# A transformer block on one core: the cell's sigmoids kept in PSUM, the output's input product made late and four tiles at once, and new instruction orders

## The reference, cut to what matters

```python
x = x + xattn0(layernorm(x), ctx, ctx, ...)   # 128 batches of 64 queries and keys, 16 heads of 8
x = x + experts(layernorm(x), ...)            # 8 experts, each token weighs its best two
x = x + xattn1(layernorm(x), ctx, ctx, ...)   # 16 heads of 8, another set of weights
x = x + cell(layernorm(x), ...)

def cell(x):                                  # x: 128 steps of 64 rows
    def step(c, xt):
        ft = sigmoid(xt @ wf.T + c @ uf.T + bf)
        it = sigmoid(xt @ wi.T + c @ ui.T + bi)
        gt = tanh(xt @ wc.T + c @ uc.T + bc)
        return ft * c + it * gt, None
    c_final, _ = lax.scan(step, c0, x)
    return tanh(einsum('tbi,oi->tbo', x, wo) + c_final @ uo.T + bo)
```

## Time and profile before

| what | value |
|---|---|
| median of 3 runs | 938.55 us (938.53 to 939.06) |
| the profiled execution | 939.48 us, span 937.7 us |
| PE busy | 875.4 us (93%) |
| PEld busy | 760.9 us (81%) |
| DVE busy | 865.1 us (92%) |
| ACT busy | 810.3 us (86%) |
| POOL busy | 624.4 us (67%) |

### The profile page before, as it was taken

One profiled execution on the slowest core, in us unless ns is written; L12 is line 12 of the kernel. 1 busy time (PEld: TensorE's weight loads), 2 busy tenths in 40 slices (PEclk: granted clock), 3 DMA queues, 4 the chain that ended last, 5 costly groups with the idle time before them and its releaser, 6 DMA issues. The chain is left out here.

```text
span 937.7 us, 37787 instructions
## 1 busy us (share of the span) xinstructions
PE 875.4 (93%) x13299; PEld 760.9 (81%) x13299; DVE 865.1 (92%) x2860; ACT 810.3 (86%) x2617; POOL 624.4 (67%) x1100
## 2 busy tenths in 40 slices
PE   6799999999999999999999999999999999999876
PEld 3588888888888888888888888888888888897652
DVE  3789999999999999999999999999999999999836
ACT  4798999999989998999899999998999899887754
POOL 5667777667766776676667666766676667656510
PEclk9899999999999999999999999999999999999988
DMA  6840000000000000000000000000000000000006
GB/s 131 229 103 2 2 2 3 3 2 3 3 3 3 2 3 3 3 2 3 3 3 3 2 3 3 3 2 3 3 3 2 3 3 3 3 2 2 3 2 179
DMA packets 37992, 17.35 MB, mean 19 GB/s; under 512 B 9176, under 2 KB 37792, under 8 KB 37808
## 3 DMA queue, kind: packets, MB, share of 16 engines
q1 hardware_dynamic: 37248, 14.67, 6.2%
q0 software_dynamic: 128, 0.07, 0.1%
q10 hardware_dynamic: 432, 0.21, 0.1%
HBM read 10.74 MB, written 4.19 MB: 16 GB/s over the span
## 5 line engine op out<-in xcount | busy, mean ns | idle before, releaser
L349 PE MATMUL ps<-cst,Ex 128*128 128x128 f32 x1024 | 163.7, 279 | 26.3 <-DVE Ex L857 25.9
L843 DVE TENSOR_REDUCE mx<-ps 128x8 f32<-128x512 f32 (+1 forms) x292 | 171.7, 611 | 11.1 <-PE ps L334 11.1
L1122 POOL TENSOR_TENSOR h<-Ex 128x512 f32<-128x512 f32 (+1 forms) x146 | 166.1, 1138 | 14.2 <-POOL h L1126 12.6
L970 DVE SCALAR_TENSOR_TENSOR acc<-ps,we,acc 128x128 f32<-128x128 f32 x448 | 155.5, 347 | 13.3
L649 ACT ACTIVATE Ex<-Ex 128x512 f32<-128x512 f32 (+1 forms) x292 | 167.4, 583 | 0.0
L660 ACT ACTIVATE ET<-ps 128x512 f32<-128x512 f32 (+1 forms) x292 | 150.8, 543 | 18.9 <-PE ps L349 18.3
L857 DVE TENSOR_TENSOR Ex<-ps,mx 128x512 f32<-128x512 f32 (+1 forms) x292 | 166.5, 609 | 0.0
L349 PEld LDWEIGHTS ps<-cst,Ex 128*128 128x128 f32 x1024 | 115.5, 142 | 38.7 <-DVE Ex L857 37.3
L418 PEld LDWEIGHTS ps<-xT,w 128*128 128x128 f32 x1024 | 123.9, 191 | 25.0 <-issue 24.8
L701 ACT ACTIVATE hT<-ps,col 128x128 f32<-128x128 f32 x512 | 139.2, 392 | 3.3 <-PE ps L418 2.9
L418 PE MATMUL ps<-xT,w 128*128 128x128 f32 x1024 | 141.1, 282 | 0.0
(11 more groups left out here) (113 smaller groups left out, 1983.4 us busy)
## 6 DMA issues: line engine op xcount, KB each, us to landing
out_dram<-x SPq DMA_DIRECT2D x15, 256.0 KB, 2.7
x<-in_x_dram SPq DMA_DIRECT2D x7, 512.0 KB, 7.2
cx<-in_ctx_dram SPq DMA_DIRECT2D x7, 512.0 KB, 7.5
w<-in_L_ffn_W_dram SPq DMA_DIRECT2D x2, 512.0 KB, 5.4
x<-in_x_dram SPq DMA_DIRECT2D x1, 256.0 KB, 3.2
cx<-in_ctx_dram SPq DMA_DIRECT2D x1, 256.0 KB, 3.5
out_dram<-x SPq DMA_DIRECT2D x2, 128.0 KB, 3.0
b<-in_L_ffn_b_dram SPq DMA_DIRECT2D x9, 4.0 KB
```

The source lines that it names most:

```text
L349: m = e.transpose(b[:, 128 * n:128 * n + 128], Ex[:, j % 2, r, 128 * n:128 * n + 128], ident)
L843: e.tensor_reduce(mx[:, j % 2, r, 4 * lo:4 * hi], b[:, 256 * lo:256 * hi].rearrange("p (j k) -> p j k", k=64), AX.X, ALU.max).then_inc(sig ...
L970: m = e.scalar_tensor_tensor(x[:, t, :] if n == 8 else d, b[:, 128 * k:128 * k + 128], we[:, t % 2, n - 1:n], d, ALU.mult, ALU.add)
L1122: e.tensor_tensor(u, v[:, :, :, 0:32], v[:, :, :, 32:64], ALU.add).then_inc(sig("half1"), 1)
```

## The change

1. The cell. `TG` is now the last 128 columns of bank 7 in PSUM. `update` is three instructions over 64 columns, each with one input from PSUM and one from SBUF. The two tanh write PSUM. Since all is in one bank, `gates` waits for the state's semaphore `C`, and `cell_inputs` waits for `C` of the previous update where it waited for `gates`.
2. The product with `wo`. ScalarE writes the fourth part of the transposed norms straight to `cx`, as an instruction of its own beside one of 128x384. `cell_inputs` reads `cx`. `out_inputs` runs only in the last sixteen groups of its stage ("W" in `SPAN`), four tiles at once: four products on TensorE and one copy of 128x512 on ScalarE. So the other groups have one product and one copy less.
3. Every engine's list has a new order, with new lags; L2 is 8, L3 is 13, and there are 79 groups. Of `USES` and the lists only a few lines are shown.
4. At the end TensorE makes the final state's product first and only then shares; `EARLY` is gone.

```diff
-L1, L2, L3 = 5, 9, 14
-LAG = {"h0": 3, "kv": 2, "sA": 2, "pv": 5, "q": 2, "e3": 4, "turnw": 3, "e1": 4, "turnx": 1, "wx": 3,
+L1, L2, L3 = 5, 8, 13
+LAG = {"pv": 5, "yb": 3, "y0": 3, "turnw": 2, "turnx": 1, "e0": 4, "wx": 2, "y1": 3, "e2": 4, "q": 2,
...
-FIRST, LAST = 0, NT + 17
+FIRST, LAST = 0, NT + 15
+SPAN = {"C": (0, NT), "N": (0, NT + L3), "A": (0, NT + L2), "F": (L1, NT), "Z": (L3, NT),
+        "W": (NT + L3 - NT // 4, NT // 4)}
...
-        xT = sb("xT", [P, 2, 4, 128])
+        xT = sb("xT", [P, 2, 3, 128])
...
-        TG = sb("TG", [P, 2, 128])
         CG = sb("CG", [P, 3, 128])
-        AB = sb("AB", [P, 2, 128])
+        ig = sb("ig", [P, 2, 64])
...
+        TG = lstm[:, 384:512]
...
             def out_inputs(i):
-                t = i - LAG["wx"] - L3
-                if not on(t):
+                j = i - LAG["wx"]
+                g = j - SPAN["W"][0]
+                if not 0 <= g < SPAN["W"][1]:
                     return
                 b = bank(i, "wx")
...
-                e.matmul(b[:, 0:128], xT[:, (t + L3) % 2, 3, :], wT[:, WX, :], start=True, stop=True).then_inc(sig("wx"), 1)
+                e.wait_ge(sig("xT"), j + 1)
+                for k in range(4):
+                    m = e.matmul(b[:, 128 * k:128 * k + 128], cx[:, 4 * g + k, :], wT[:, WX, :], start=True, stop=True,
+                                 skip_group_check=True)
+                m.then_inc(sig("wx"), 1)
...
-                    e.wait_ge(sig("gates"), 2 * t)
+                    e.wait_ge(sig("C"), 2 * t + 1)
...
+                end = min(hi, 3)
+                if lo < end:
+                    m = e.activation(xT[:, j % 2, lo:end, :],
+                                     b[:, 128 * lo:128 * end].rearrange("p (k n) -> p k n", k=end - lo), ACT.Copy)
+                if hi == 4:
+                    m = e.activation(cx[:, j - L3, :], b[:, 384:512], ACT.Copy)
+                m.then_inc(sig("xT"), 1)
...
                 e.wait_ge(sig("z"), k + 1)
-                if k >= 2:
-                    e.wait_ge(sig("AB"), k - 1)
-                e.activation(TG[:, k % 2, 0:64], lstm[:, o:o + 64], ACT.Tanh, bias=col[:, BF + 4:BF + 5])
-                e.activation(TG[:, k % 2, 64:128], lstm[:, 128 + o:192 + o], ACT.Tanh, bias=col[:, BF + 5:BF + 6])
+                e.wait_ge(sig("C"), k + 1)
+                e.activation(TG[:, 0:64], lstm[:, o:o + 64], ACT.Tanh, bias=col[:, BF + 4:BF + 5])
+                e.activation(TG[:, 64:128], lstm[:, 128 + o:192 + o], ACT.Tanh, bias=col[:, BF + 5:BF + 6])
...
-                e.scalar_tensor_tensor(AB[:, k % 2, :], TG[:, k % 2, :], 1.0, CG[:, k % 3, :],
+                e.scalar_tensor_tensor(TG[:, 0:64], TG[:, 0:64], 1.0, CG[:, k % 3, 0:64], ALU.add, ALU.mult)
+                e.scalar_tensor_tensor(ig[:, k % 2, :], TG[:, 64:128], 1.0, CG[:, k % 3, 64:128],
                                        ALU.add, ALU.mult).then_inc(sig("AB"), 1)
                 e.wait_ge(sig("AB"), k + 1)
-                e.scalar_tensor_tensor(CG[:, (k + 1) % 3, 0:64], AB[:, k % 2, 0:64], 0.5, AB[:, k % 2, 64:128],
+                e.scalar_tensor_tensor(CG[:, (k + 1) % 3, 0:64], TG[:, 0:64], 0.5, ig[:, k % 2, :],
                                        ALU.mult, ALU.add).then_inc(sig("C"), 1)
...
             for k in range(len(mine)):
-                if k >= EARLY:
-                    if k >= 7:
-                        e.wait_ge(sig("tanh"), [n for n, (adder, _) in enumerate(TAIL) if adder == "pe"][k - 7] + 1)
-                    share(k, 0)
                 share(k, 1).then_inc(sig("pre_pe"), 1)
+                if k >= 6:
+                    e.wait_ge(sig("tanh"), [n for n, (adder, _) in enumerate(TAIL) if adder == "pe"][k - 6] + 1)
+                if k + 1 < len(mine):
+                    share(k + 1, 0)
```

More of the change, by code:

```diff
@@ L496, in tensor_program @@
                     turn_weights(i - FIRST - 5)
-                hidden(i, 0)
-                keys_values(i)
-                step(i, 0)
                 values(i)
-                query(i)
-                turn_e(i, 3)
-                turn_w(i)
-                turn_e(i, 1)
-                turn_x(i)
-                out_inputs(i)
-                project(i)
                 expert_bias(i)
                 experts(i, 0)
+                turn_w(i)
+                turn_x(i)
+                turn_e(i, 0)
+                out_inputs(i)
+                experts(i, 1)
                 turn_e(i, 2)
-                turn_r(i)
+                query(i)
                 gate(i)
                 ctx_turn(i)
-                experts(i, 1)
-                turn_e(i, 0)
+                project(i)
+                hidden(i, 0)
+                turn_e(i, 3)
+                turn_e(i, 1)
                 step(i, 1)
@@ L519, in tensor_program @@
                 cell_inputs(i)
+                turn_r(i)
+                keys_values(i)
+                step(i, 0)
             mine, lo = [], 0
@@ L531, in share @@
                                 skip_group_check=True)
-            for _, reader, _, chain, step, first in USES:
-                e.wait_ge(sig(reader), step * (SPAN[chain][1] - 1) + first)
-            for k in range(EARLY):
-                share(k, 0)
             e.wait_ge(sig("C"), 2 * NT + 1)
@@ L1008, in vector_program @@
                     bias_pieces()
+                differences(i, 2)
+                maxima(i, 3)
+                differences(i, 3)
+                combine(i, 0)
+                normal(i)
+                combine(i, 1)
+                combine(i, 2)
+                stats_inputs(i)
+                combine(i, 3)
+                update(i, 0)
+                combine(i, 4)
+                combine(i, 5)
+                combine(i, 6)
                 combine(i, 7)
+                gate(i)
                 combine(i, 8)
+                gate_top(i)
+                sums(i)
+                gate_index(i)
+                project(i)
+                gate_float(i)
+                inverse(i)
+                stats_attention(i)
+                stats_experts(i)
+                gate_weights(i)
+                spread(i)
+                update(i, 1)
                 maxima(i, 0)
[L1012 removed]
                 maxima(i, 1)
                 differences(i, 0)
+                maxima(i, 2)
                 differences(i, 1)
[L1016 to L1040 removed]
             e.wait_ge(sig("uo"), 1)
@@ L1044, in vector_program @@
             e.wait_ge(sig("cU"), 1)
-            e.wait_ge(sig("xo"), NT)
+            e.wait_ge(sig("xo"), NT // 4)
             lo = [sum(n for _, n in TAIL[:k]) for k in range(len(TAIL) + 1)]
```

108 lines of the change are left out of this document (38 added, 70 removed), and 30 rows, old and new, of tables (LAG, USES).

## The result

The changed kernel takes **902.1 us** (median of 4 runs, 901.12 to 904.01), beside 938.8 us of the kernel before (now of 4 runs): a ratio of 0.9608 (0.9589 to 0.9627 with 95%). The forecast was 899.0 in a range of 889 to 918. The profiled run took 901.91 us, with a span of 900.0.

A forecast was written before the change was run, and what follows sets the result against it. VectorE, its updates blocked by GpSimd, was taken as the bound, TensorE next. Span 937.7 - 27.1 - 15.7 + 2.6 - 2.0 + 5.0 - 2.5 = 898.0, plus 1.8 less 0.9: 899 us, range 889 to 918.

The forecast's parts named there:

- full groups, i = 15 to 63: 49 full groups at 12.6 us against 644.5 us before: -27.1 us.
- drain, i = 64 to the last state: Drain: one group less, late products +2.6, VectorE's faster update -2.0, cell inputs waiting for the state +5.0 us.
- end: After the last state: final product first brings cU 3.5 us sooner, ScalarE's first share about 1 us late; -2.5 us.
- step 2: Product with wo leaves full groups: 0.22 us less TensorE work, putting TensorE's floor at 12.52 us, or 12.66.
- Step 1: Cell's update through PSUM: 0.57 us each, no meeting with GpSimd; VectorE's need falls by 0.98 to 12.46 us a group.
- the forecast's mechanism: Full groups: TensorE just above its floor sets the pace; chance 0.60, between 892 and 907 us.
- Step 3: Full groups, new orders: three engines within 0.4 us, hand-offs cost something; group of 12.6 us (12.5 to 12.9).
- the moved collision: Rival: another VectorE instruction with two SBUF inputs, or a conversion, meets GpSimd's sums; groups of 13.1, 923 us; chance 0.12.
- VectorE's relief: First three groups of the drain, still VectorE's: -0.7 us each from the cheaper update, -2.0 us.
- the dependent cell with one group less: Drain's late groups: input products wait for the state and updates lengthen, +5.0 us, with one group of 6.89 us saved.
- VectorE at its high price: Rival: VectorE stays the bound at 12.76 us a group, 12.85 with hand-offs; 911 us; chance 0.15.
- the loop past its break-even: Rival: gates, update and score instructions delay TensorE's banks by over 1.0 us a group; 945 us at 1.1; chance 0.05.

The follow-up runs named there:

- e12: Kernel before with only the update through PSUM, plus the second update moved ahead of the first maximum in VectorE's list: 901.88 us, groups of 12.57.
- e4: Changed kernel with the cell's update back in SBUF, cell inputs waiting for the gates only: 919.36 us, groups of 13.04.
- e10: Changed kernel with VectorE's statistics of the inputs moved from between two experts' sums to behind the reciprocal: 900.78 us, groups of 12.47.
- e5: Changed kernel with the product with wo made one tile in each group again, read from cx: 900.44 us, groups of 12.63.
- e6: Changed kernel with one more, unread 128x128 product on TensorE before the gate's in each of 64 groups: 916.98 us, groups of 12.77.
- e7: Changed kernel with one more, unread statistics instruction on VectorE in each of 64 groups: 914.59 us, groups of 12.74.
- e1: Kernel before with only the cell's update through PSUM, old orders and lags: 930.09 us, groups of 13.09.
- e3: Kernel before with the update through PSUM and the late product with wo, old orders, lags and end: 929.89 us.
- e8: Changed kernel with the end of the kernel before, two shares ahead of the final state's product: 907.51 us.

## Why the prediction was right, and where not

The time was in the range and 3.1 us above the point. By its own steps (span; the terms of the drain taken together):

```
us                                  predicted  measured
fill, one group less                     -8.8     -10.1
full groups, i = 15 to 63               -27.1     -28.8
drain, i = 64 to the last state          -1.3      +3.5
end                                      -2.5      -2.3
```

That the sum came so near is in part luck: the drain's 4.8 us too little were made good by 3.0 too much in the fill and the full groups, and the group's length was right for a wrong reason (step 2).

**What bounds the kernel: right.** VectorE set the pace through updates that GpSimd blocked. e12 shows it by itself: with the PSUM update and its place in the list the group falls by 0.86 us. e4 shows the block come back with SBUF, once a group; its 13.04 against before's 13.43, with the second update undisturbed, shows too that the other changes take away part of the blocking without PSUM.

**Step 1: right, a little too dear.** Taken 0.57 us an update, measured 0.53; 0.14 from start to start where the inputs are ready. The rule of the Trainium skill, page "VectorE: DVE Perf Modes", section on the TRN2 errata, of 120 cycles plus the columns would be about 0.19 as an estimate. It gave a bound of 12.85, and the runs have 12.53 and 12.47, so the measurement decides against it. VectorE's need of 12.46 was met to 0.01 in e10.

**Step 2 and the forecast's mechanism: wrong, at nearly the right number.** The floor of 12.52 for TensorE was taken from the short group in which PE showed 12.88 of 12.88 busy. A busy share of one doesn't exclude waits, as overlapping records cover them. And that group still had half of the stall: only L984 was short there, while L981 took its 0.93 us. DVE in before, ahead of the earlier trace rows:

```profile
549.54 0.93 DVE L981 SCALAR_TENSOR_TENSOR AB<-TG,CG 128x128 f32<-128x128 f32 x1
```

L984's 0.54 us less (0.77 to 0.23) are nearly the whole difference of 0.56 from 13.44, so VectorE can have set the pace there too, and the 12.88 say only that TensorE needs no more. e5 puts its work without the product at 12.41 or less, and e6, e7 and e10 show that a loop through both engines stood at 12.53. The prediction weighed one loop, through the banks of the scores, as a rival at 0.05 (by its own 4.9 us for each 0.1 its 945 should be 943). It missed this tighter one, which goes on through the experts' sums and the query's bank. The product taken out was worth 0.08 us a group and not 0.22, some 4 us, as much as it costs in the drain: that is why moving it there gained nothing.

**Step 3, the orders: the failed step is what they are for.** I read them as hand-offs of 0.1 us and counted the new wait of the cell's inputs for the update in the drain alone, not in a full group. The old order made this cost 0.5 us a group (e1 against e12), as much as the moved collision would have. The chosen orders cure it, so the sum didn't suffer; my expectation for e1 and e3 did, by 19 and 24 us.

**The drain: the mis-sized terms.** Its product was put at +2.6 in about four groups, with -2.0 from VectorE's relief in three. Measured over i = 64 to 70 is 79.8 us against 75.0: +4.8 instead of +0.6. The eight groups from i = 63 on, in one line of the stretches view of after:

```profile
sum 93.11, PE 92.17 PEld 82.83 DVE 82.16 ACT 82.99 POOL 60.53; mean PE 11.52 PEld 10.35 DVE 10.27 ACT 10.37 POOL 7.57
```

PE is busy for 92.17 of 93.11 us, and the runs show who pays. Beside e5, which has three products fewer in each of these groups, after is longer by 0.65 to 0.68 us in five of them (i = 63 to 67, the first of which the prediction counts as a full group) and by 0.25 to 0.36 in the next three. From i = 64 on that makes 3.7 us instead of 2.6. The relief is the larger miss: e5 is still 1.1 us longer than before over i = 64 to 70, where -2.0 was forecast, and after is no shorter over i = 63 to 70 than e4, from which it differs in the update alone (93.1 and 92.3). In the old orders the relief came at first and was paid back: e12 is 1.4 us shorter than before over i = 64 to 66 and 1.4 longer over i = 67 to 70. What holds up these last four groups was not looked for. The rest of the drain, the dependent cell with one group less, was put at -1.9 and came as -1.3 (+5.0 for the new wait; e4 without that wait is 4 us shorter there). In the chain's last groups it stands in the waits of PE of after, beside the earlier trace rows:

```profile
873.33 0.91 PE L476 MATMUL ps<-cx,wT 128*128 128x128 f32 x6 [1.56 <-DVE CG L991]
```

The text allowed the drain, from i = 64 to the last state, 5 us of growth; it was 3.5.

**The end: right in size, its cause shown in part.** Beside the earlier trace rows, DVE in order of time in after:

```profile
877.97 0.23 DVE L991 SCALAR_TENSOR_TENSOR CG<-ps,ig 128x64 f32<-128x64 f32 x1
878.73 0.29 DVE L1050 TENSOR_TENSOR cU<-ps,bo 128x128 f32<-128x128 f32 x1 [0.54 <-PE ps L539]
...
883.69 1.30 DVE L1065 TENSOR_TENSOR x<-cx,x 128x512 f32<-128x512 f32 x2 [1.95 <-ACT cx L787]
```

cU comes 0.76 us after the last state, not 5.07. Of the 4.3 us gained, 1.95 go back where VectorE waits for ScalarE's tanh of TensorE's first chunk, whose shares stand behind the product now and run at a granted clock of 0.70 (the fifth stretch above). How much the new order gives by itself stays open: e8 against after says 0.8, and with the old order the end took from 22.8 (e8) to 24.5 us (e12), with the new one from 20.4 (e4) to 23.3 (e7).

**The rivals.** VectorE at its high price (911), the moved collision (923) and the loop past its break-even (945) didn't come; no instruction of VectorE's update is above 0.23 us. Of the signs named, the group of 12.6, PE's full share, VectorE's 0.1 to 0.2 idle at the second gates and cU within 2 us all came; one of them, VectorE idle while TensorE is full, was the mark of the loop, which I took for that of a TensorE bound.

## What to carry to other kernels

A VectorE instruction with two SBUF inputs that meets GpSimd's work can be freed by putting one input in PSUM; then look at what the new place makes wait, and move the instruction it waits for ahead in the list, since here this swap was worth more than all the rest of the orders. Work moved from the loop into the drain is free only where its engine idles there, and what it is worth in the loop is known only after a small instruction has been added on each engine: if additions on two engines both cost in full, a loop through both is the limit and neither engine's busy share tells it. Measure waits from start to start, as busy 100% doesn't exclude them. And look at which parts of a stall are missing in a short group before you read its length as another engine's floor.

## What the runs showed of the hardware

- On VectorE, 64 columns with one PSUM and one SBUF input pass in 0.14 us from start to start (465.24 to 465.38) and a dependent one in 0.24 with its gap. Reading PSUM showed no extra price beside 0.15 for 64 columns from SBUF alone, L984 of before in the first half step (503.81, then 503.96 in the earlier trace rows):

```profile
503.81 0.23 DVE L984 SCALAR_TENSOR_TENSOR CG<-AB 128x64 f32<-128x64 f32 x1
```

- An instruction of VectorE with two SBUF inputs of 128 columns grew from 0.28 to 0.79 us and ended just after GpSimd's (e4); one of 64 columns with one input in PSUM stayed at 0.22 beside the same instruction (after).
- TensorE's granted clock in a drain in which PE is busy for about 70% differs between executions of the same instructions: from i = 71 to the last state 50.6 us in after, at 1.00, and 55.0 in e8, where 45 us of it show 0.88, thus part of the time at 1.2 instead of 2.4 GHz. These 4.4 us are more than several of the edits were worth. e12, with other orders, had 0.67 over 30 us. What tips it is open.
